# A two-layer graph network on one core: loads alternated at the end of layer 1, evictions taken first, and the counts' second part moved from GpSimd to VectorE

## The chip, the core and the metric

The kernel runs on one core of one Trainium2 chip. The core has TensorE (PE, matrix products into PSUM), VectorE (DVE), ScalarE (ACT), GpSimd (POOL), and SyncE (SP), which here issues nearly all DMA transfers. Each engine works through its own list of instructions in order and waits on semaphores; the DMA engines, 16 of them, are shared. The metric is device microseconds of one execution, lower is better.

## What is computed

`x` has 2500 rows of 1024; there are 80000 edges with a source, a target (sorted) and a weight.

```python
edge_index = jnp.stack([src, dst])
h = jnp.maximum(_layernorm(x), 0.0)
x = x + segment_sum((h @ W0)[src] * edge_weight[:, None], dst)      # layer 1
h = jnp.maximum(_layernorm(x), 0.0)
# layer 2: row, col = src, dst with one self loop for each node
h = einsum('nd,od->no', h, W1) + b
deg = zeros(N).at[row].add(1.0)
norm = deg[row] ** -0.5 * deg[col] ** -0.5
x = x + segment_sum(norm[:, None] * h[col], row)
```

## The kernel before

Both sums over edges are done as dense products. From the edge list the kernel builds two matrices of 2500 x 2500: the weighted adjacency of layer 1 and the edge counts of layer 2. Float32 accuracy comes from pairs of float16 numbers, a first part and what is left over, so each product is three matmuls.

**Quads.** A tile is 128 rows of the result; there are T = 20. A tile's matrix rows are built in 8 quads of 16 rows (QPT = 8, 160 quads in all). For a quad, POOL writes the fields of its edges (`fields_of`, `own_step`), DVE turns them into one-hot columns (`one_hots`, four instructions), PE multiplies these (L1695) into a PSUM pair that holds counts and weights. Then comes the eviction: ACT's `window_out` (L1413 to L1415) reads three pieces out of PSUM, DVE's `second_part` adds the self loop (L1118, which signals `c_self`) and forms the second part of the weights (L1119, L1122). PE may reuse the PSUM pair once L1119 has signalled `win_evac`. The counts are then handled in three steps: POOL adds them to the degrees (`sum_counts`, L774), ACT writes their first part (`counts_first`, L1420, signals `c_hi`), and POOL subtracts it to get the second part (`counts_left`, L779, signals `c_lo`). SP stores both parts to DRAM (`c_scratch`), to be read back transposed in layer 2.

**Stages.** (1) Support: 20 steps of `h @ W0` on PE; in the 16 steps w = 0 to 15 from step 4 on, one quad each is built beside them and parked in DRAM by SP (`park_quad`). SP also stores the split weights of layer 2 there (`store_w1`; ACT's `split_block` L1448 waits for an earlier one of these stores before it overwrites the staging buffer), and DVE takes the moments of x (`support_share`, L867). (2) The loop over tiles: PE adds up tile td (`dense`, L1796, 120 matmuls in 8 pieces) and builds the quads of tile td + 1 between the pieces. Up to quad 63 a window holds 2 rows (r = 2, six such tiles in the loop), after that 4 (r = 4, eleven tiles). DVE does the one-hots of quad n, then the second part of quad n - 1, then at q = 2 `residual` and at q = 4 `moments_of_x1`, then `further`, which loads a register from `quad_tab` (L1069) and branches. (3) The seam: after the last tile SP waits for the stores of the counts, issues five transposing loads of the counts' first parts (`load_first_parts`, L581), then stores a tile of x1, then loads x1 in groups of four tiles (`load_x1`, L591), and later two transposing loads of the second parts (`load_second_parts`, L586). ACT normalises each x1 tile (L1604), DVE splits it (L1297), and PE's `sums_of_first` (L1883) takes x1 tile k with quarter k // 4 of the transposed counts. Over on POOL the degrees are written to DRAM (L844, 2560 single numbers of 4 bytes) and read back in another layout (L847); DVE needs them at its ninth split. (4) Layer 2: five chunks of 500 rows on PE.

What sets the order is the text of each engine's program; nothing is scheduled by a planner. A wait holds everything behind it on its engine, and SP's transfers go out in SP's order.

Of the kernel before, what the change touches and what calls it, by code (L numbers as in the profile page):

```python
# [6 lines left out]
def gnn_two_layers(nc, x, src, dst, edge_weight, w0, w1, b1, out):  # L7
    f32, i32, f16 = mybir.dt.float32, mybir.dt.int32, mybir.dt.float16
    ALU = mybir.AluOpType
# [60 lines left out]
    with ctx:  # L70
# [394 lines left out]
        def _(sp):  # L465
# [59 lines left out]
            for w in range(PQ):  # L525
# [96 lines left out]
            sp.wait_ge(agg_ready, T)  # L622
# [57 lines left out]
        def _(pool):  # L680
# [95 lines left out]
            def counts_left(n, s, first_parts, second_parts):  # L776

                pool.wait_ge(c_hi, n + 1)
                pool.tensor_tensor(second_parts, by_source(c_stage(s)), first_parts, ALU.subtract).then_inc(c_lo, 1)  # L779

            def counts_of(n, td, q, first=False):

                sum_counts(n, q % CST)
                if not first:
                    last_left(n - 1, (q - 1) % QPT)

            def last_left(n, q):

                at = slice(q % QH * RQ, (q % QH + 1) * RQ)
                half = c_half(q // QH)  # L790
                counts_left(n, q % CST, half[:, 0, :, at], half[:, 1, :, at])

            def early_sum(n):
                sum_counts(n, n % 2)

            def early_left(n):
                counts_left(n, n % 2, c_parts[:, 0], c_parts[:, 1])

            pool.wait_ge(more_consts, 3)
            fields_of(0)  # L800
            for t in range(STEP0, T):
# [3 lines left out]
                if w < PQ:  # L805
                    if w > 0:
                        early_sum(w - 1)
# [5 lines left out]
                    if w > 0:  # L813
                        early_left(w - 1)
# [3 lines left out]
            early_sum(PQ - 1)  # L818
            early_left(PQ - 1)

            def own_tile(td, r, first=False):

                for q in range(QPT):
# [5 lines left out]
                    counts_of(n, td, q, first=first and q == 0)  # L829

            own_tile(PRE, 2, first=True)
# [1152 lines left out]
```

## Time and profile before

| | us |
|---|---|
| median of 3 runs | 1503.33 |
| lowest, highest | 1501.31, 1504.87 |
| the profiled execution | 1509.67 |
| its span, first to last instruction | 1507.9 |
| PE busy | 1422.7 (94%) |
| DVE busy | 896.9 (59%) |
| ACT busy | 507.4 (34%) |
| POOL busy | 453.9 (30%) |

All durations come from that one profiled execution. Busy PE is no measure of PE at its peak, but idle PE on the chain that ends last is time lost. Idle time of another engine costs nothing unless PE waits for it.

### The profile page before, as it was taken

To read this page: it belongs to the slowest core of one execution; us is meant where nothing else is said; L and a number is where in the kernel's file an instruction comes from. 1 tells how busy PE (TensorE), PEld (TensorE's weight loads), DVE (VectorE), ACT (ScalarE), POOL (GpSimd) and SP (SyncE) were. 2 spreads that over 40 slices of the span, in tenths; PEclk is the share of its full clock that TensorE was granted. 3 is DMA by queue.
4 is the path that set the end of the run, shared out by engine and by line. 5 is a ranking of instruction groups with operands and counts; after the bars stand their busy time and mean duration, and the time that the engine had idled before them with its cause. 6 is when DMAs were issued, how large, how long until landed. Compare 5 with 4: busy or idle time off the path is not lost.

```text
span 1507.9 us, 23949 instructions
## 1 busy us (share of the span) xinstructions
PE 1422.7 (94%) x7586; PEld 845.5 (56%) x7587; DVE 896.9 (59%) x1804; ACT 507.4 (34%) x922; POOL 453.9 (30%) x867
## 2 busy tenths in 40 slices
PE   3989988999999999999999994799999999999999
PEld 2445444556666666666666662346546446446455
DVE  7787775653767776776677760784452452452542
ACT  7545555532444444555455440710000000000000
POOL 2246444642555555555555540000000000000000
PEclk9989999999999999999999997899999999999999
DMA  8302424151434545545454559926308109108002
GB/s 304 113 20 47 102 47 90 20 90 49 96 78 80 85 78 103 94 80 102 85 95 84 103 88 101 304 73 131 119 1 206 44 1 209 40 21 201 28 2 82
DMA packets 422945, 139.17 MB, mean 92 GB/s; under 512 B 392832, under 2 KB 405120, under 8 KB 422796
## 3 DMA queue, kind: packets, MB, share of 16 engines
q1 hardware_dynamic: 422588, 137.41, 41.9%
q8 instruction: 60, 0.98, 0.3%
q0 software_dynamic: 208, 0.04, 0.2%
q14 instruction: 89, 0.73, 0.2%
HBM read 53.46 MB, written 53.52 MB: 71 GB/s over the span
## 4 chain that ended last, share of the span: by engine, by line
PE 72%; issue 8%; DVE 7%; SPq 4%; DMA 4%; POOL 3%; ACT 2%; POOLq 1%; ACTq 0%; DVEq 0%
PE pair L1796 24%; PE pair L1883 23%; PE pair L1943 13%; PE pair L1683 7%; PE pair L1695 4%; SPq L581 2%; DMA h<-in_x 1%; DMA w_scratch<-aux 1%; DVE stats L867 1%; SPq L508 1%; DMA h<-x_scratch 1%; DVE slots L1051 1%; POOL deg_acc L774 1%; DVE own_w L1360 1%; POOL fbuf L767 0%
## 5 line engine op out<-in xcount | busy, mean ns | idle before, releaser
L1796 PE MATMUL pair<-h,area 128*128 128x512 f16 x2400 | 542.7, 379 | 0.0
L1796 PEld LDWEIGHTS pair<-h,area 128*128 128x128 f16 x2400 | 342.6, 146 | 147.5
L1883 PE MATMUL pair<-area,h 128*128 128x500 f16 x1600 | 340.7, 376 | 30.7 <-DVE h L1297 30.7
L1883 PEld LDWEIGHTS pair<-area,h 128*128 128x128 f16 x1600 | 157.2, 98 | 213.5 <-issue 34.8
L774 POOL TENSOR_TENSOR deg_acc<-deg_acc,area 128x320 f32<-128x320 f32 x160 | 139.5, 872 | 273.3 <-DVE area L1118 271.8
L1943 PE MATMUL pair<-wmat,area 128*125 128x512 f16 x960 | 209.0, 379 | 0.0
L1617 ACT ACTIVATE area<-pair,sc 128x500 f16<-128x500 f32 x40 | 27.1, 677 | 452.4 <-PE pair L1883 452.4
L1413 ACT ACTIVATE area<-pair 128x320 f32<-128x320 f32 x160 | 70.0, 438 | 318.1 <-PE pair L1695 310.7
L1943 PEld LDWEIGHTS pair<-wmat,area 128*125 128x125 f16 x960 | 130.7, 137 | 75.5
L779 POOL TENSOR_TENSOR aux<-area,aux 128x320 f16<-128x320 f32 x144 | 147.7, 1026 | 0.0
L1695 PE MATMUL pair<-slots 128*128 128x120 f16 (+1 forms) x1152 | 112.9, 235 | 23.6 <-DVE area L1119 12.2
L1420 ACT ACTIVATE aux<-area 128x320 f16<-128x320 f32 x144 | 126.6, 879 | 0.0
L1695 PEld LDWEIGHTS pair<-slots 128*128 128x128 f16 x1152 | 84.9, 99 | 71.2 <-DVE slots L1055 23.8
L1049 DVE TENSOR_TENSOR slots<-iota_r,fbuf 128x320 f16<-128x320 f16 (+1 forms) x145 | 66.2, 456 | 93.2 <-POOL fbuf L768 47.5
L1683 PE MATMUL pair<-wmat,aux 128*128 128x512 f16 x480 | 116.4, 392 | 3.1 <-DVE wmat L943 3.1
L1683 PE MATMUL pair<-wmat,xt 128*128 128x512 f16 x480 | 113.9, 388 | 0.4 <-DVE h L956 0.3
L1122 DVE TENSOR_TENSOR area<-area 128x320 f16<-128x320 f16 x160 | 109.7, 686 | 5.5
L1340 DVE SCALAR_TENSOR_TENSOR area<-pair,sc,area 128x500 f16<-128x500 f32 x40 | 29.5, 739 | 128.9 <-ACT area L1617 128.9
L1051 DVE TENSOR_TENSOR slots<-iota_r,fbuf 128x1024 f16<-128x1024 f16 x145 | 101.0, 696 | 0.0
L1118 DVE TENSOR_TENSOR area<-area 128x16 f16 (+1 forms) x160 | 32.1, 200 | 101.8 <-ACT area L1415 99.6
L1683 PEld LDWEIGHTS pair<-wmat,aux 128*128 128x128 f16 x480 | 46.5, 100 | 54.2 <-issue 8.6
L1119 DVE SCALAR_TENSOR_TENSOR area<-pair,area 128x320 f16<-128x320 f32 x160 | 76.6, 479 | 0.0
(210 smaller groups left out, 1254.9 us busy)
## 6 DMA issues: line engine op xcount, KB each, us to landing
c_scratch<-aux SPq DMA_DIRECT2D x72, 320.0 KB, 4.5
xt<-in_x SPq DMA_DIRECT2D x19, 512.0 KB, 3.5
x_scratch<-xt SPq DMA_DIRECT2D x19, 512.0 KB, 4.7
xt<-x_scratch SPq DMA_DIRECT2D x20, 448.0 KB
out_x<-xt SPq DMA_DIRECT2D x19, 448.0 KB
h<-x_scratch SPq DMA_DIRECT2D x4, 2048.0 KB, 17.2
h<-in_x SPq DMA_DIRECT2D x5, 1024.0 KB, 7.8
h<-in_L_gnn_W SPq DMA_DIRECT2D x4, 1024.0 KB, 11.1
```

The lines of the kernel that those rows point to most:

```text
L774: pool.tensor_tensor(deg_acc[:], deg_acc[:], c_stage(s), ALU.add).then_inc(win_sum, 1)
L779: pool.tensor_tensor(second_parts, by_source(c_stage(s)), first_parts, ALU.subtract).then_inc(c_lo, 1)
L1051: nc.vector.tensor_tensor(part(to, 0, P), columns(8, P), by_touch(s, 1, 8, P), ALU.is_equal)
L1119: nc.vector.scalar_tensor_tensor(by_window(parts[:, 1], r), sums_in(pair, r, 1), A_DOWN, by_window(parts[:, 0], r), ALU.mult, ALU.subtract ...
L1122: nc.vector.tensor_tensor(parts[:, 1], parts[:, 1], seconds, ALU.add).then_inc(win_lo, 1)
L1413: act.activation(by_window(c_stage(s), r), sums_in(pair, r, 0), ACT.Copy, scale=C_DOWN)
L1420: act.activation(to, by_source(c_stage(s)), ACT.Copy).then_inc(c_hi, 1)
L1683: last = pe.matmul(dest[:, half * H:(half + 1) * H], h_t(t)[:, q, k, :], wmat[:, r, k, half * H:(half + 1) * H], start=k == q == r == 0, s ...
L1695: return pe.matmul(dest, touches[:, t, 0:P], touches[:, t, P:], start=first, stop=last, skip_group_check=True)
L1796: last = pe.matmul(sum_pair(e)[:, half * H:(half + 1) * H], wts(e)[:, q, :, k], hpart(k, r)[:, half * H:(half + 1) * H], start=k == q == r ...
L1883: ins = pe.matmul(sums_of(c, f), hpart(k, q)[:, f * P:(f + 1) * P], counts, start=first and q == 0, stop=last and q == 1, skip_group_check ...
L1943: last = pe.matmul(out_pair(m)[0:RW, half * H:(half + 1) * H], agg_of(k, q)[:, b * RW:(b + 1) * RW], wmat[:, r, k, half * H:(half + 1) * H ...
```

## The change

- `counts_left` leaves POOL and becomes DVE's: in the loop it follows the next quad's second part (`left_of(n - 2, q - 2)`), with two of them at a tile's end; in the support stage it is `early_left(w - 1)` just ahead of `early_second_part(w)`.
- DVE's order in a support step: quad w's second part now comes in step w, ahead of moments and selections, and the first one-hots of quad w + 1 come ahead of it. Before, it came in step w + 1. ACT's square roots (`std`) follow its `window_out` there.
- At a tile's end DVE does the last second part ahead of the next tile's first one-hots, and ACT the last first part inside the same tile.
- SP: the counts' parking is split off as `park_counts` and comes behind the weight stores and x loads of the step. At the seam the tile of x1 is stored first, the two degree transfers are SP's and not POOL's, and the loads of first parts and of x1 alternate.

```diff
@@ SP
                 sp.wait_ge(win_lo, n + 1)
                 for z in range(2):
                     sp.dma_start(a_dram[z, n], parked[:, z]).then_inc(a_out, 16)
+
+            def park_counts(n):
+
                 sp.wait_ge(c_lo, n + 1)
...
+                if w > 0:
+                    park_counts(w - 1)
             sp.wait_ge(sup_out, T)
             sp.dma_start(xt[:, 0, :], x[0:P, :]).then_inc(xt_in[0], 16)
             park_quad(PQ - 1)
+            park_counts(PQ - 1)
...
             sp.wait_ge(agg_ready, T - 1)
+            store_x1(last, 0)
+            sp.wait_ge(deg_ready, 1)
+            sp.dma_start(deg_dram.rearrange("t p -> p t"), deg[:, 0:T], allow_slow_non_contiguous=True).then_inc(deg_out, 16)
             sp.wait_ge(win_lo, NQ)
             sp.wait_ge(c_out[0], 32 * (PQ + T - PRE))
             sp.wait_ge(c_out[1], 32 * (T - PRE))
-            for j in range(HJ):
-                load_first_parts(0, j)
-            store_x1(last, 0)
+            load_first_parts(0, 0)
             for s in range(2):
                 sp.wait_ge(x1_out[s], 16 * last)
             for k in range(4):
                 sp.wait_ge(sup_free, k + 1)
                 load_x1(k)
+                load_first_parts(0, k + 1)
+                if k == 0:
+                    sp.wait_ge(deg_out, 16)
+                    flat = deg_dram.rearrange("t p -> (t p)")
+                    sp.dma_start(deg[0:RW, T:2 * T], flat[0:N].rearrange("(t p) -> p t", p=RW),
+                                 allow_slow_non_contiguous=True).then_inc(degu_in, 16)
@@ DVE
+            def counts_left(n, s, first_parts, second_parts):
+
+                dve.wait_ge(c_hi, n + 1)
+                nc.vector.tensor_tensor(second_parts, by_source(c_stage(s)), first_parts, ALU.subtract).then_inc(c_lo, 1)
...
+                    if q > 1:
+                        left_of(n - 2, q - 2)
...
                 n = QPT * (td + 2)
+                second_part(n - 1, r, quad_of(1 - e, QPT - 1), second_of(1), win_pair(1), c_stage((QPT - 1) % CST), td + 1, QPT - 1)
+                left_of(n - 2, QPT - 2)
                 own_hots(n + PRE_STEPS - PQ if r == 2 else (QPT // 2) * (td + 2) + QB // 2 + PRE_STEPS - PQ, 0,
                          n - 1 + PRE_STEPS - PQ if r == 2 else steps_used(n - 2), after)
-                second_part(n - 1, r, quad_of(1 - e, QPT - 1), second_of(1), win_pair(1), c_stage((QPT - 1) % CST), td + 1, QPT - 1)
+                left_of(n - 1, QPT - 1)
...
             for w in range(PQ):
-                if w > 0:
-                    hots_of(w, 0, 1)
-                    early_second_part(w - 1)
-                    hots_of(w, 1, 2)
+                hots_of(w, 1, 2) if w > 0 else None
                 sup_left(w + STEP0 - 1)
                 hots_of(w, 2, 8)
                 for g in W1_AT.get(w + STEP0, ()):
                     split_left(g)
-                support_share(w)
                 if w + STEP0 == HOTS_AT:
                     chunk_one_hots()
+                further(w, 2)
+                if w + 1 < PQ:
+                    hots_of(w + 1, 0, 1)
+                if w > 0:
+                    early_left(w - 1)
+                early_second_part(w)
+                support_share(w)
@@ ACT
                 if 0 <= w < PQ:
-                    if w in MOMENTS_AT:
-                        std(MOMENTS_AT[w])
                     if w > 0:
                         early_counts_first(w - 1)
                     early_window_out(w)
+                    if w in MOMENTS_AT:
+                        std(MOMENTS_AT[w])
```

POOL loses `counts_left` in both stages and the two degree transfers.

How it moves instructions, at three places. In these rows a name in brackets is a semaphore that is waited for.

SP in the support stage, two steps, of before: a quad's weights parked (L505), its counts (L508), then the weight stores of layer 2 (L496).

```order
L505 DMA a_scratch<-area 128x320 [waits win_lo]
L505 DMA a_scratch<-area 128x320
L508 DMA c_scratch<-area 128x20x16 [waits c_lo]
L508 DMA c_scratch<-area 128x20x16
L496 DMA w_scratch<-aux 128x2x512 [waits wlo_ready] x2
```

The same place of after:

```order
L505 DMA a_scratch<-area 128x320 [waits win_lo]
L505 DMA a_scratch<-area 128x320
L496 DMA w_scratch<-aux 128x2x512 [waits wlo_ready] x2
L511 DMA c_scratch<-area 128x20x16 [waits c_lo]
L511 DMA c_scratch<-area 128x20x16
```

The wait for `c_lo` and the two stores of counts have moved behind the weight stores.

DVE in the r = 2 part of the loop, the end of a tile, of after (L1028 to L1034 are the one-hots, L1097 to L1101 the second part, L1106 the moved subtraction):

```order
L1097 TENSOR_TENSOR area<-area 128x16 [waits win_act]
L1098 SCALAR_TENSOR_TENSOR area<-pair,area 128x320
L1101 TENSOR_TENSOR area<-area 128x320 [waits win_evac]
L1105 REGISTER_ALU
L1106 TENSOR_TENSOR aux<-area,aux 128x20x16 [waits c_hi]
L1043 ISA
L428 REGISTER_ALU [waits own_fields]
L1028 TENSOR_TENSOR slots<-iota_r,fbuf 128x8x40 [waits step_used]
L1030 TENSOR_TENSOR slots<-iota_r,fbuf 128x8x128
L1032 REGISTER_ALU
L1033 TENSOR_TENSOR slots<-slots,fbuf 128x8x40 [waits hots_plain]
L1034 TENSOR_TENSOR slots<-slots,fbuf 128x8x40
```

and a quad inside a tile of before, from its one-hots to the register load of `further`:

```order
L1049 TENSOR_TENSOR slots<-iota_r,fbuf 128x8x40 [waits step_used,own_fields]
L1051 TENSOR_TENSOR slots<-iota_r,fbuf 128x8x128
L1053 REGISTER_ALU
L1054 TENSOR_TENSOR slots<-slots,fbuf 128x8x40 [waits hots_plain]
L1055 TENSOR_TENSOR slots<-slots,fbuf 128x8x40
L1116 REGISTER_ALU
L1118 ISA [waits win_act]
L1118 TENSOR_TENSOR area<-area 128x16
L1119 SCALAR_TENSOR_TENSOR area<-pair,area 128x320
L1122 TENSOR_TENSOR area<-area 128x320 [waits win_evac]
```

A wait for `c_hi` and one more instruction have come behind each second part, and at a tile's end the one-hots stand behind the last second part.

SP at the seam, of before:

```order
L581 DMA_TRANSPOSE area<-c_scratch 128x4x512 [waits c_out0,c_out1,win_lo,agg_ready]
L581 DMA_TRANSPOSE area<-c_scratch 128x4x512 x4
L557 DMA x_scratch<-xt 128x1024 [waits x1_ready]
L591 DMA h<-x_scratch 128x4x1024 [waits sup_free,x1_out1,x1_out0]
L591 DMA h<-x_scratch 128x4x1024 [waits sup_free] x3
L591 DMA h<-x_scratch 128x3x1024 [waits x1_out0,agg_ready]
```

and of after:

```order
L563 DMA x_scratch<-xt 128x1024 [waits x1_ready,agg_ready]
L619 DMA deg_scratch<-deg 128x20x1 [waits deg_ready]
L587 DMA_TRANSPOSE area<-c_scratch 128x4x512 [waits c_out1,c_out0,win_lo]
L597 DMA h<-x_scratch 128x4x1024 [waits sup_free,x1_out1,x1_out0]
L587 DMA_TRANSPOSE area<-c_scratch 128x4x512
L633 DMA deg<-deg_scratch 125x20x1 [waits deg_out]
L597 DMA h<-x_scratch 128x4x1024 [waits sup_free]
L587 DMA_TRANSPOSE area<-c_scratch 128x4x512
L597 DMA h<-x_scratch 128x4x1024 [waits sup_free]
L587 DMA_TRANSPOSE area<-c_scratch 128x4x512
```

The first x1 load has one transposing load ahead of it and not five, and both degree transfers have come into SP's list: the write ahead of every transposing load, the read ahead of the second x1 load.

## Rows read from the trace of the kernel before

**Rows 1.** Windows: length, busy us by engine (instructions), clock, DMA share, GB/s.

```profile
170.00:210.00 40.00, 33.66 (x223) 17.83 (x221) 32.27 (x68) 18.76 (x31) 18.68 (x46) 0.96 0.30 59
210.00:252.00 42.00, 33.69 (x221) 17.77 (x220) 25.08 (x63) 22.98 (x37) 18.20 (x51) 0.96 0.46 94
```

**Rows 2.** The chain that ended last, support stage: start, us, what.

```profile
197.15 0.78 POOL area L779
...
199.76 4.42 DMA w_scratch<-aux
...
233.45 7.83 DMA h<-in_x
...
248.09 0.98 PE pair L1695 x8
```

**Rows 3.** Waits of PE, 60 to 330 us: total, times, longest.

```profile
PE pair L1695 <- DVE area L1119: 12.2, 4, 5.9
```

**Rows 4.** Timeline of the r = 2 loop: start, us, instruction, idle before it.

```profile
454.24 0.86 POOL L774 TENSOR_TENSOR deg_acc<-deg_acc,area 128x320 f32<-128x320 f32 x1 [2.37 <-DVE area L1118]
...
455.06 1.02 POOL L779 TENSOR_TENSOR aux<-area,aux 128x320 f16<-128x320 f32 x1
...
456.50 0.33 DVE L1049 TENSOR_TENSOR slots<-iota_r,fbuf 128x320 f16<-128x320 f16 x1 [1.22 <-POOL fbuf L768]
...
457.82 0.18 DVE L1118 TENSOR_TENSOR area<-area 128x16 f16 x1
...
458.43 0.70 DVE L1122 TENSOR_TENSOR area<-area 128x320 f16<-128x320 f16 x1
```

**Rows 5.** The chain, whole span: a tile's last piece of 25 matmuls.

```profile
508.46 5.42 PE pair L1796 x25
...
539.39 5.41 PE pair L1796 x25
...
568.59 5.40 PE pair L1796 x25
```

**Rows 6.** Timeline, 882 to 1010 us: two DVE instructions.

```profile
889.47 0.49 DVE L1049 TENSOR_TENSOR slots<-iota_r,fbuf 128x640 f16<-128x640 f16 x1 [0.85 <-issue]
...
896.40 0.81 DVE L1258 TENSOR_REDUCE deg<-deg_acc 128x20 f32<-128x320 f32 x1
```

**Rows 7.** Windows over the seam, columns as in rows 1.

```profile
920.00:940.00 20.00, 1.43 (x7) 0.71 (x5) 0.00 (x0) 0.00 (x0) 3.02 (x1) 0.67 1.21 139
940.00:960.00 20.00, 7.83 (x26) 3.13 (x27) 8.84 (x15) 11.54 (x11) 0.00 (x0) 0.57 1.01 392
```

**Rows 8.** Timeline of the seam.

```profile
897.79 1.54 POOL L844 DMA_DIRECT2D deg_scratch<-deg  x1 [3.50 <-DVEq L1260]
...
900.51 36.41 SPq L581 DMA_TRANSPOSE area<-c_scratch  x5
...
952.17 58.14 PE L1883 MATMUL pair<-area,h 128*128 128x500 f16 x263 [30.74 <-DVE h L1297]
```

**Rows 9.** The chain across the seam and behind it.

```profile
937.66 10.62 DMA h<-x_scratch
...
952.17 70.17 PE pair L1883 x320
```

**Rows 10.** DMA issues, 880 to 1010 us: KB each, median us from issue to landing.

```profile
wmat<-w_scratch SPq DMA_TRANSPOSE x1, 24.5
deg_scratch<-deg POOLq DMA_DIRECT2D x1, 10.0 KB, 24.4
deg<-deg_scratch POOLq DMA_DIRECT2D x1, 9.8 KB, 15.5
```

**Rows 11.** All 25 issues of L581: issue ns min/median/max, then landing us.

```profile
L581 SPq DMA_TRANSPOSE area<-c_scratch x25: 1882/2257/13646, 900.5 to 1361.0; - x25
...
DMA to landing us min/median/max: 4.4/4.8/23.2
```

**Rows 12.** All 72 issues of L522, 2560 pieces of 128 bytes each: landing us.

```profile
DMA to landing us min/median/max: 3.4/4.5/5.7
```

More of the change, by code:

```diff
@@ L774, in sum_counts @@
                 pool.tensor_tensor(deg_acc[:], deg_acc[:], c_stage(s), ALU.add).then_inc(win_sum, 1)
[L776 to L797, printed above, removed]
             pool.wait_ge(more_consts, 3)
@@ L806, in _ @@
                     if w > 0:
-                        early_sum(w - 1)
+                        sum_counts(w - 1, (w - 1) % 2)
                     if w + 1 < PQ:
@@ L817, in _, with own_tile @@
                     pool.memset(h[:, T - 1, :], 0.0).then_inc(pad_done, 1)
-            early_sum(PQ - 1)
-            early_left(PQ - 1)
-            def own_tile(td, r, first=False):
+            sum_counts(PQ - 1, (PQ - 1) % 2)
+            def own_tile(td, r):
                 for q in range(QPT):
@@ L828, in own_tile @@
                         own_step((QPT // 2) * td + q // 2 + 1 + QB // 2 + PRE_STEPS - PQ, (q // 2 + 1) % 2)
-                    counts_of(n, td, q, first=first and q == 0)
-            own_tile(PRE, 2, first=True)
-            with pool.Fori(PRE + 1, QB // QPT) as td:
+                    sum_counts(n, q % CST)
+            with pool.Fori(PRE, QB // QPT) as td:
                 own_tile(td, 2)
@@ L840, in _ @@
                              of=PRE_STEPS if q == QPT - 2 else None)
[L841 to L848 removed]
+                sum_counts(QPT * td + q, q % CST)
         @block.vector
@@ L1122, in second_part, with left_of, early_left @@
                 nc.vector.tensor_tensor(parts[:, 1], parts[:, 1], seconds, ALU.add).then_inc(win_lo, 1)
+            def counts_left(n, s, first_parts, second_parts):
+                dve.wait_ge(c_hi, n + 1)
+                nc.vector.tensor_tensor(second_parts, by_source(c_stage(s)), first_parts, ALU.subtract).then_inc(c_lo, 1)
+            def left_of(n, q):
+                at = slice(q % QH * RQ, (q % QH + 1) * RQ)
+                half = c_half(q // QH)
+                counts_left(n, q % CST, half[:, 0, :, at], half[:, 1, :, at])
+            def early_left(n):
+                counts_left(n, n % 2, c_parts[:, 0], c_parts[:, 1])
             def early_second_part(n):
@@ L1428, in early_window_out, with tile, first_of @@
                 window_out(n, n % 2, 2, 2, parked[:, 0], early_second, WIN)
-            def tile(td, e, r, before=True):
+            def tile(td, e, r):
+                def first_of(n, p):
+                    b = p // QH
+                    if p % QH == 0:
+                        act.wait_ge(c_out[b], (32 * PQ if b == 0 else 0) + 32 * (td + 1 - PRE))
+                    counts_first(n, p % CST, c_half(b)[:, 0, :, p % QH * RQ:(p % QH + 1) * RQ])
                 for q in range(QPT):
@@ L1436, in tile @@
                     window_out(n, q % CST, r, CST, quad_of(1 - e, q)[:, 0], second_of(q % 2), win_pair(q % 2))
-                    if q > 0 or before:
-                        p = (q - 1) % QPT
-                        b = p // QH
-                        if p % QH == 0:
-                            act.wait_ge(c_out[b], (32 * PQ if b == 0 else 0) + 32 * (td + 1 - PRE))
-                        counts_first(n - 1, p % CST, c_half(b)[:, 0, :, p % QH * RQ:(p % QH + 1) * RQ])
+                    if q > 0:
+                        first_of(n - 1, q - 1)
+                first_of(n, QPT - 1)
             def split_block(g):
@@ L1578, in _ @@
                 act.wait_ge(w_out[k], 16 * KD)
-            tile(1, 1, 2, before=False)
+            tile(1, 1, 2)
             tile(2, 0, 2)
```

14 lines of the change are left out of this document (1 added, 13 removed).

## The prediction
> **What bounds the kernel now.** I first read the windows of busy time over the whole span. In the r = 4 part of the loop and in layer 2 PE goes from matmul to matmul, so nothing can be won there but by shorter PE work, and the change has none. PE idles in three places, and each was then followed in the chain that ended last, in the waits and in the timeline.
>
> The first is the support stage. From 170 to 252 us PE is busy 33.66 and 33.69 us of 40 and 42, so it idles 6.3 + 8.3 = 14.7 us [rows 1]. 12.2 us of PE's waits in this stage are for DVE's L1119, the release of the PSUM pair [rows 3]. The chain shows why it is late: POOL's subtraction L779, then SP's stores, then a weight store of 4.42 us to its landing, then ACT and DVE; later a load of x that SP issued only behind all this, 7.83 us, at whose end PE resumes at 248.09 [rows 2]. So the eviction of a quad hangs on a subtraction that nobody there needs, because SP and ACT work in order.
>
> The second is the r = 2 part of the loop. From 508.46 to 539.39 a tile takes 30.93 us, or 3.87 per quad; the next one, r = 4, takes 29.20 [rows 5]. In the r = 2 timeline DVE stands idle 1.22 us before its one-hots, waiting for POOL, and POOL has just spent 1.02 us on L779 [rows 4]. The loop that sets the pace is DVE L1118, POOL L774, POOL L779, POOL's copies, DVE's one-hots. From 456.50 to 457.82 these take 1.32 us, and L1122 starts 0.61 after L1118 [rows 4].
>
> The third is the seam. PE is busy 1.43 us of the window from 920 and resumes at 952.17 [rows 7, 8]: 30.7 us idle. ACT's first x1 group, issued at 937.66, landed 10.62 us later [rows 9]; SP had spent 36.41 us from 900.51 on five transposing loads ahead of it [rows 8]. Undisturbed, such a load takes 2.26 us to issue and 4.8 to land [rows 11]. Here everything is slow together: a weight transpose took 24.5 us, and so did (24.4) the degree write, issued at 897.79, which puts its landing at 922.2; the degree read after it took 15.5 [rows 8, 10]. The size of the pieces alone isn't it: the count stores, also 2560 pieces but of 128 bytes and far apart, land in 4.5 [rows 12]. I read it as the 4-byte numbers, all in 10 KB of DRAM, holding up the others.
>
> **Support stage.** The wait for `c_lo` goes behind the weight stores and the x loads on SP, the subtraction goes to DVE, and DVE evicts quad w ahead of moments and selections. The 14.7 us [rows 1] lose their cause. Against it: DVE is busy 32.27 us of 40 [rows 1], gets an instruction more, and now waits inside step w for quad w's last matmul and ACT's eviction, with moments and selections pushed between that and the next quad's second one-hots. Those are four steps with moments and eight with selections; I charge 3.7 us for them, as a guess between 0 and 10 us. ACT's square root now comes after DVE's late moments, and ACT's next work queues behind it; PE is a whole support step away from that, so nothing is charged. Gain 11 us; bounds 4 (14.7 less the 10) and 16 (14.7 and the clock, 0.96 in both windows, back to 1).
>
> **Loop, r = 2.** Without L779 POOL's loop falls below 3 us and DVE's own becomes the longest. How long is the moved instruction on DVE? The trace has none, but L1258 reads the same strided view of 320 numbers in 0.81 us [rows 6]; dense float16 of that size takes 0.33 [rows 4], POOL 1.02. I take 0.81. Behind L1122 DVE's sequencer loads a register: L1049 came after 0.85 us of idle at the end of a 0.70 us L1122, so 1.55 from start to start [rows 6]. The new instruction hides in that gap, but its wait and dispatch lengthen it by some 0.15. A quad costs 1.32 + 0.61 + 1.70 = 3.63 us, eight 29.0. At q = 2 and q = 4 the gap was already filled by residual and moments, so there the instruction and the longer fill show, about 1.0 each, and two subtractions at the tile's end show 0.4: 31.4 us. That is 0.5 more than 30.93, times six tiles +3 us. Bounds: with 0.33 us nothing shows and PE's 29.2 holds, -10; with 1.02 us +8. I keep +2, a little below the sum, because the first part's POOL wait also goes from the tile end.
>
> The Trainium skill ("VectorE: DVE Perf Modes", the section on the TRN2 errata) gives a float32 `tensor_tensor` as (N + 151)/0.96 ns, which by estimate is 0.49 us for 320 numbers; by it the r = 2 tiles would come out at about 30.3 us and the stage 4 us faster, not 2 slower. The strided L1258 at 0.81 speaks against using it here, and no run yet shows which holds.
>
> **Loop, r = 4.** A tile is PE's 29.20 us [rows 5]. DVE has 28 us or so to do, by the same sum with one-hots only every second quad. The tight place is the tile's end: the next tile's one-hots now follow the last second part. PE works 5.4 us on its last piece [rows 5]; DVE needs an estimated 1.3 until ACT has evicted, 0.61, 0.62 for L1122, 0.81, and 1.8 for the wider one-hots (1.32 and three times 0.16, from L1049's 0.49 and 0.33 [rows 4, 6]): 5.1 us. It just fits. I charge 1 us for eleven tiles; bounds 0 and +7 (0.6 us each).
>
> **The seam.** In the new order SP stores the counts about 1 us later (two subtractions stand behind each other on DVE), loads the last weights, stores x1 and issues the degree write near 903.5, an estimate from 900.51 [rows 8] and these. If the write holds up the queue as before, for some 21 us, it ends near 925. Part of the first transposing load trickles in meanwhile and lands at 927. One x1 group follows, 2.1 MB at 392 GB/s [rows 7] or 5.3 us: 932. From the landing at 948.28 to PE at 952.17 it took 3.9 us [rows 8, 9], so PE resumes near 936, not 952: 16 us won. Then the read of degrees, 15.5 us [rows 10], stands ahead of the second x1 group, which lands about 948; PE needs it split by 936 + 14 = 950, at 14.0 us a group (70.17 / 5 [rows 9]), and has it near 952 to 956. I charge 4. Seam: -12 us. Later groups come every 10 us or so and PE takes 14; the rest is hidden.
>
> **The sum.** -11 + 2 + 1 - 12 = -20 us. The profiled execution took 1509.67 us with a span of 1507.9, 6 above the median; 20 off the median of 1503.33 gives **1483 us**. Its own range, with the small bounds, is 1474 to 1493.
>
> **The rivals.**
> 1. *The write holds up nothing when SP issues it.* For it: the count stores land in 4.5 us from the same queue [rows 12], and the slow write was POOL's only one of its kind. Against it: what stood still were SP's transfers, not POOL's. Then the first loads are in by about 915, PE resumes at its own end, 921.4, and 31 us are won for 12: 1464 us.
> 2. *Support stage wins nothing.* DVE's wait for quad w takes the place of PE's wait for the release, and PE waits for one-hots instead. For it: DVE 81% busy. Against it: PE's idle time is tied to the chain of SP, not to DVE's load. 1494 us.
> 3. *DVE sets the pace of the loop.* If the moved instruction takes 1.02 us or meets POOL's L774, r = 2 gives +8 and r = 4 +7: 1503.33 - 11 + 15 - 12 = 1495; with the low support gain of 4, 1502.
> 4. *The degree read blocks SP's queue: slower.* It has 125 rows of 20 numbers, all single, and stands ahead of three quarters of x1; the kernel itself cuts other 125-row transfers into 112 and 13. If it runs on a few DMA engines, say five, each has 500 numbers. The read before took 15.5 us for some 156 per engine, 0.10 us each, and the write 24.4 for 160, 0.15 [rows 10]: 50 us, up to 76. With 50 the second group lands at 988, PE starts on it at 992 and ends the sums at 1048, against 952.17 + 70.17 = 1022.3: +26 where I have -12. 1503.33 - 8 + 26 = 1521 us. It decides from a read of some 32 us on: then the seam loses the 8 us which the rest wins.
>
> The Trainium skill ("DMA: Bandwidth & Descriptors", the section on why a DMA increments its semaphore by 16) says that a transfer from SP runs on the largest number of engines up to 16 that divides the slowest dimension, which is five for 125 rows. If it holds, rival 4's premise stands, though not its price per number. No transfer shown here tells it.
>
> **How the numbers follow.** Forecast 0.45; rival 1 0.20; rival 2 0.10; rival 3 0.15; rival 4 0.10. About 0.2%, 3 us, is what a measurement of this kernel can tell from no change. The range 1458 to 1502 us takes in rivals 1 to 3 and leaves out rival 4 and the far ends of the rest. Faster by over 0.2% 0.86, within 0.04 (the upper end of rival 3), slower 0.10 (rival 4).
>
> **What would show it.** Support: the wait of L1695 for the second part below 3 us, a weight store never between POOL and ACT in the chain, PE's idle time from 170 to 252 us near 4. Loop: the moved instruction at 0.7 to 0.9 us; r = 2 tiles at 31 to 31.5 us with DVE and no longer POOL named before PE's gaps, r = 4 at 29.2 to 29.4. Seam: the degree write landing after 20 us or more and PE resuming near 936 with a short second gap; a landing within 6 us is rival 1, a gap of over 30 us before x1's second group rival 4. The forecast is wrong if the seam is off by more than 8 us in either direction, or if r = 4 tiles grow.

## The result and the profile after

| | before | after |
|---|---|---|
| median us | 1504.43 | 1499.85 |
| lowest, highest | 1501.31, 1509.06 | 1497.14, 1502.39 |
| span of the profiled execution | 1507.9 | 1498.6 |

The ratio is 0.997, 95% interval 0.9957 to 0.9983: the change wins 4.6 us, with 2.6 to 6.5 inside the interval, where 20 had been forecast. The two profiled spans differ by 9.3 us; the profile of before lies some 5 us above its median, so sizes below are taken from timed runs where there are some, and from the traces for the place.

By stages the traces give: first tiles 3.7 us earlier, r = 2 the same, r = 4 slower by 7.8, and the seam shorter by 13.4 (from the end of the last dense piece to the 144 matmuls of layer 2 in a row behind it).

**Support stage.** The windows that answer to [rows 1]:

```profile
170.00:210.00 40.00, 35.20 (x230) 18.63 (x229) 35.15 (x75) 20.84 (x34) 17.32 (x44) 0.91 0.33 50
210.00:252.00 42.00, 42.00 (x288) 23.05 (x287) 28.96 (x66) 26.68 (x42) 22.35 (x59) 1.00 0.39 76
```

PE's idle time in these two windows falls from 14.7 to 4.8 us, and the wait of [rows 3] is gone. What PE waits for at its window matmuls, 60 to 330 us, is now the one-hots (L1034 in after):

```profile
PE pair L1697 <- DVE slots L1034: 12.6, 4, 4.9
```

In before PE waited 12.2 us there for the second part and 4.5 for one-hots, 16.7 together, so the waits of the stage as a whole fall by only 4.1. One of the four, 2.98 us at 104.88, is in before as well. The longest of the four is new, from PE's timeline:

```profile
298.93 0.98 PE L1697 MATMUL pair<-slots 128*128 128x120 f16 x8 [4.87 <-DVE slots L1034]
```

DVE's timeline tells what it did meanwhile. L1098 is the eviction of quad 12; L1218 to L990 is `later_windows`, a table for the loop; L1028 begins quad 13's second one-hots:

```profile
284.44 0.34 DVE L1028 TENSOR_TENSOR slots<-iota_r,fbuf 128x320 f16<-128x320 f16 x1 [5.84 <-POOL fbuf L771]
...
286.60 0.48 DVE L1098 SCALAR_TENSOR_TENSOR area<-pair,area 128x320 f16<-128x320 f32 x1
...
287.35 0.68 DVE L1218 CAST area<-area 1x768 f32<-1x768 int32 x1
...
296.39 1.23 DVE L990 TENSOR_TENSOR area<-area 1x768 int32<-1x768 f32 x1
297.50 0.30 DVE L1028 TENSOR_TENSOR slots<-iota_r,fbuf 128x320 f16<-128x320 f16 x1
```

The table takes 10.2 us. Before the change it stood ahead of an eviction; now it stands between one and the next one-hots, while DVE had just been idle for 5.84 us.

Two more of the four waits, 1.60 us at 181.21 and 3.10 at 193.99, have something else in common. Ahead of both a one-hot instruction that has a median of 0.32 us took 2.2, and it ended together with POOL's L737, which ran beside it:

```profile
177.45 2.62 POOL L737 TENSOR_TENSOR xt<-h,xt 128x1024 f16<-128x1024 f32 x1 [9.60 <-ACT xt L1468]
...
178.00 2.26 DVE L1033 TENSOR_TENSOR slots<-slots,fbuf 128x320 f16<-128x320 f16 x1
...
190.52 2.33 POOL L737 TENSOR_TENSOR aux<-h,aux 128x1024 f16<-128x1024 f32 x1 [4.01 <-ACT aux L1468]
...
190.79 2.24 DVE L1033 TENSOR_TENSOR slots<-slots,fbuf 128x320 f16<-128x320 f16 x1
```

Ahead of the second of them DVE also had a block of selections, 3.8 us from 185.96. Before has such long one-hots too (2.25 us at 116.26, 130.84 and 180.44, among others), so they are no effect of the change; no run here moves L737, so that it is the cause is not shown, and what it costs was not measured.

**The loop.** The moved instruction, from the groups of DVE instructions:

```profile
L1106 DVE TENSOR_TENSOR aux<-area,aux 128x320 f16<-128x320 f32 x144 | 116.0, 805 | 0.0
```

At r = 2, from 382 to 535 us, DVE no longer waits for POOL ahead of its one-hots. In before that was

```profile
DVE slots L1049 <- POOL fbuf L768: 32.6, 28, 1.2
```

and in after

```profile
DVE slots L1028 <- POOL fbuf L781: 0.5, 1, 0.5
```

In its place DVE has more to do: it is busy 141.1 us of these 153 and not 113.7. One has eaten up the other. Five tiles, from the first to the last r = 2 piece, take 156.4 us in both kernels.

The last pieces of r = 4 tiles in the chain, to be compared with [rows 5]:

```profile
564.86 5.39 PE pair L1798 x25
...
625.67 5.39 PE pair L1798 x25
...
685.68 5.39 PE pair L1798 x25
...
745.70 5.40 PE pair L1798 x25
```

Two tiles take 60.8, 60.0 and 60.0 us where before two took 58.4. PE waits at every second tile's start only (five times, 5.8 us in all), where DVE's loop, whose body holds two tiles, goes round. The timeline there:

```profile
598.98 0.81 DVE L1106 TENSOR_TENSOR aux<-area,aux 128x320 f16<-128x320 f32 x1
...
605.59 0.49 DVE L1028 TENSOR_TENSOR slots<-iota_r,fbuf 128x640 f16<-128x640 f16 x1 [5.81 <-issue]
...
607.50 0.48 DVE L1098 SCALAR_TENSOR_TENSOR area<-pair,area 128x320 f16<-128x320 f32 x1
...
608.11 0.58 PE L1697 MATMUL pair<-slots 128*128 128x240 f16 x4 [2.03 <-DVE area L1098]
```

Nothing that the profile shows was waited for in those 5.81 us; in the chain they hold two stretches called issue, of 2.30 and 2.28 us (1.3 to 2.1 each at the later boundaries). The kernel before has the same gap at the same place, and PE loses nothing by it:

```profile
663.51 0.49 DVE L1049 TENSOR_TENSOR slots<-iota_r,fbuf 128x640 f16<-128x640 f16 x1 [4.54 <-issue]
```

What differs is where the gap begins. In before DVE's last instruction ahead of it ends 3.0 us after PE's last piece has begun (658.97 against 655.96), in after 5.9 (599.79 against 593.88).

**The seam.** The timeline of SP, and PE's resuming, which answer to [rows 8]:

```profile
903.73 0.51 SPq L563 DMA_DIRECT2D x_scratch<-xt  x1
904.29 0.43 SPq L619 DMA_DIRECT2D deg_scratch<-deg  x1
905.20 11.57 SPq L587 DMA_TRANSPOSE area<-c_scratch  x1
916.88 0.51 SPq L597 DMA_DIRECT2D h<-x_scratch  x1
917.44 12.96 SPq L587 DMA_TRANSPOSE area<-c_scratch  x1
930.45 0.48 SPq L633 DMA_DIRECT2D deg<-deg_scratch  x1
930.97 3.65 SPq L597 DMA_DIRECT2D h<-x_scratch  x1
934.52 55.48 PE L1885 MATMUL pair<-area,h 128*128 128x500 f16 x256 [8.99 <-DVE h L1296]
```

The degree write landed after 18.6 us. PE's gap is 8.99 us where it was 30.7. Behind it PE is busy throughout until 990, but then waits 3.2 and 4.0 us more; before had no such waits there. The granted clock from 1010 to 1025 us, behind them, is 0.81.

### The profile page after: what moved, and what is told of

The parts are those of the page before. It is cut to its first block, busy times and chain, and to the rows that moved or that the text cites. A ratio compares the mean times of both kernels' runs of the same rounds, so it can differ in the third digit from the quotient of the medians.

```text
span 1498.6 us, 24031 instructions
## 1 busy us (share of the span) xinstructions
PE 1426.0 (95%) x7586; PEld 845.8 (56%) x7587; DVE 1000.8 (67%) x1964; ACT 509.6 (34%) x922; POOL 356.6 (24%) x705
## 4 chain that ended last, share of the span: by engine, by line
PE 55%; issue 20%; DVE 9%; POOL 5%; SPq 5%; POOLq 2%; DMA 1%; ACT 1%; DVEq 1%
PE pair L1885 18%; PE pair L1798 17%; PE pair L1945 13%; SPq L587 3%; PE pair L1697 3%; PE pair L1685 3%; DVE own_w L1359 2%; POOL fbuf L781 2%; POOLq L766 1%; POOL fbuf L769 1%; POOL fbuf L771 1%; SPq L592 1%; POOL deg_acc L787 1%; DVE stats L846 1%; DVE slots L1033 1%
## 5 line engine op out<-in xcount | busy, mean ns | idle before, releaser
L1885 PE MATMUL pair<-area,h 128*128 128x500 f16 x1600 | 339.7, 375 | 12.2 <-DVE h L1296 9.0
L1619 ACT ACTIVATE area<-pair,sc 128x500 f16<-128x500 f32 x40 | 27.1, 677 | 450.1 <-PE pair L1885 450.1
L1106 DVE TENSOR_TENSOR aux<-area,aux 128x320 f16<-128x320 f32 x144 | 116.0, 805 | 0.0
L1101 DVE TENSOR_TENSOR area<-area 128x320 f16<-128x320 f16 x160 | 107.9, 674 | 5.5
L1028 DVE TENSOR_TENSOR slots<-iota_r,fbuf 128x320 f16<-128x320 f16 (+1 forms) x145 | 56.6, 391 | 69.7 <-POOL fbuf L771 27.6
L1098 DVE SCALAR_TENSOR_TENSOR area<-pair,area 128x320 f16<-128x320 f32 x160 | 76.5, 478 | 0.0
L1685 PEld LDWEIGHTS pair<-wmat,xt 128*128 128x128 f16 x480 | 46.1, 99 | 52.0 <-issue 4.3
## 6 DMA issues: line engine op xcount, KB each, us to landing
h<-x_scratch SPq DMA_DIRECT2D x4, 2048.0 KB, 10.3
```

What stands on the lines that cost most here:

```text
L1098: nc.vector.scalar_tensor_tensor(by_window(parts[:, 1], r), sums_in(pair, r, 1), A_DOWN, by_window(parts[:, 0], r), ALU.mult, ALU.subtract ...
L1101: nc.vector.tensor_tensor(parts[:, 1], parts[:, 1], seconds, ALU.add).then_inc(win_lo, 1)
L1106: nc.vector.tensor_tensor(second_parts, by_source(c_stage(s)), first_parts, ALU.subtract).then_inc(c_lo, 1)
L1685: last = pe.matmul(dest[:, half * H:(half + 1) * H], h_t(t)[:, q, k, :], wmat[:, r, k, half * H:(half + 1) * H], start=k == q == r == 0, s ...
L1885: ins = pe.matmul(sums_of(c, f), hpart(k, q)[:, f * P:(f + 1) * P], counts, start=first and q == 0, stop=last and q == 1, skip_group_check ...
```

## The experiments

A line "start of tiles" below is the time from the first of PE's transposes in the support stage to the first 25-matmul piece; it takes out that the traces begin up to 2 us apart.

**1. The seam alone.** The kernel before, with this at the seam and POOL's two degree transfers taken out:

```diff
-            for j in range(HJ):
-                load_first_parts(0, j)
             store_x1(last, 0)
+            sp.wait_ge(deg_ready, 1)
+            sp.dma_start(deg_dram...)
...
+            load_first_parts(0, 0)
...
                 load_x1(k)
+                load_first_parts(0, k + 1)
```

> The kernel before with the seam of after alone: x1's tile stored first, both degree transfers from SP, loads of first parts and of x1 alternating. Theory (the three parts add up, the seam wins its 13 us by itself): 1504.4 - 13 = 1491 us, the support stage and the loop as in the kernel before to within 1 us, PE resuming at 9 us after its last dense piece. Rival (the seam wins only because the loop before it ends later and so hides part of the degree write, 4 us): 1495 us, and the gap of PE 13 us or more.

1493.19 us, ratio 0.9922 (0.99 to 0.9943), halfway between theory and rival; PE's gap of 9.40 us is the theory's. The seam wins 11 us by itself. So the rest of the change loses 6.7.

**2. The table ahead.** `later_windows` moved ahead of `further` in its step:

```diff
+                if w + STEP0 == TABLE_AT:
+                    later_windows()
                 further(w, 2)
...
-                if w + STEP0 == TABLE_AT:
-                    later_windows()
```

> After, with the table of the later windows (13 instructions, 10.2 us on DVE) moved ahead of further and of the next quad's first one-hots in step w = 12, where DVE stands idle 5.84 us. Theory (the stall of 4.87 us at 298.9 and the low clock behind it are this table, standing between quad 12's eviction and quad 13's second one-hots): the stall goes, the support stage ends 5 to 6 us earlier, 1499.9 - 5.5 = 1494.4 us. Rival (DVE's load as a whole is the limit of this stage, the table only shows it first): the stall moves to the next step or two, and 1 us or less is won, 1499.

1493.42 us, ratio 0.9929 (0.9907 to 0.9952), 6.4 us below after. The stall of 4.87 us is replaced by two short ones in PE's timeline:

```profile
287.73 0.59 PE L1697 MATMUL pair<-slots 128*128 128x120 f16 x8 [0.67 <-DVE area L1098]
...
291.99 0.59 PE L1697 MATMUL pair<-slots 128*128 128x120 f16 x8 [1.08 <-DVE slots L1034]
```

Start of tiles: 321.3 and 321.0 us in before and the first experiment, 314.9 to 317.5 in the kernels with after's support stage (after itself is the highest), 309.9 here. With the table out of the way the support stage wins 11 us in this trace. The three kernels further down that have the same edit start their tiles at 309.5, 310.7 and 313.2, so a single trace gives this size to some 3 us; the 6.4 us are timed.

**3. The tile's end.** The next tile's one-hots ahead of the last second part again:

```diff
+                own_hots(...)
                 second_part(n - 1, ...)
                 left_of(n - 2, QPT - 2)
-                own_hots(...)
                 left_of(n - 1, QPT - 1)
```

> After, with the tile's end of the kernel before in DVE's order: the next tile's one-hots ahead of the last second part, the two subtractions last; they stay on DVE. Theory (the r = 4 loop lost 7.8 us because the tile's end is too long ahead of the loop's branch: four one-hot instructions now stand between the last eviction and the rest): nothing of the one-hots' 1.8 us is waited for behind the last eviction, 3 to 6 us come back, 1494 to 1497 us. Rival (the end's order is of no matter, what counts is what DVE has to do before its branch, the last subtraction with its wait for ACT): 1500 us, each second tile still 1 us or more over 29.2.

1497.31 us, ratio 0.9954 (0.9935 to 0.9974), its interval overlapping with after's. In the trace four waits for L1098 of 5.3 us in all remain at the boundaries (after: five, 5.8 us). The order of the end is not the cause, or only a small part: r = 4 as a whole is 0.8 us shorter than in after.

**4. No loop.** DVE's r = 4 tiles written out one after the other, the same instructions:

```diff
-            with dve.Fori(j + 1, last) as j:
+            for j in range(j + 1, last):
```

> After, with DVE's loop over the r = 4 tiles written out (ten tiles in a row, no branch back); all else, and all instructions of each tile, as in after. Theory (the loss sits at every second tile's end only, where DVE branches back and is idle 5.8 us before it goes on): the stalls of 1.2 to 2.0 us at each second boundary vanish, r = 4 takes 377 to 378 us and not 384.4, 1499.9 - 7 = 1493 us. Rival 1 (DVE simply has too much to do at a tile's end): the stalls stay and spread over all boundaries, 1500. Rival 2 (straight code must be fetched too, and costs DVE more than one branch): stalls at other places, 1500 or slower.

1489.6 us, ratio 0.991 (0.9885 to 0.9935), 10 us below after. The chain:

```profile
562.25 5.40 PE pair L1798 x25
591.43 5.40 PE pair L1798 x25
620.61 5.40 PE pair L1798 x25
```

29.18 us for each tile, no wait at a boundary. With the same work at each tile's end the loss is gone, so DVE's load alone is not the cause; the way round the loop is. The DMA lists show a queue of instructions, number 14: 95 packets over the whole of after, 89 in before, 77 here. The Trainium skill ("Runtime: NRT & Kernel Launch", the section "Instruction fetch mechanics") says that a taken branch out of the window of prefetched instructions forces a fetch before the engine goes on; that agrees with an idle DVE of 5.8 us that waits for nothing, and with its vanishing here. That each of the two stretches of 2.3 us is one such fetch is argued, not shown; what is shown is that the idle time belongs to the loop.

**5. DVE's second part first.** At q = 1 of an r = 4 tile, `second_part` ahead of `own_hots`, still in the loop:

```diff
                         elif q % 2 == 1 and q < QPT - 1:
+                            if q == 1:
+                                second_part(n - 1, ...)
                             own_hots(...)
-                        second_part(n - 1, ...)
+                        if r == 2 or q != 1:
+                            second_part(n - 1, ...)
```

> After, with DVE taking the second part of quad 0 ahead of the one-hots at q = 1 in the r = 4 tiles; the loop stays a loop. Theory (PE waits at every second tile for this one instruction, which stands 1.8 us of one-hots behind the end of DVE's branch): the waits for L1098 vanish or fall below 0.3 us each, r = 4 takes 379 us or less, not 384.4, 1499.9 - 6 = 1494 us. Rival (the one-hots are as urgent, and PE waits for them at the next quad instead): waits of the same 1 to 2 us, now for L1034, 1499 to 1501 us.

1502.24 us, ratio 0.9988 (0.9977 to 0.9999). The theory's remedy failed, as the rival said. The idle time stands where it stood, and PE waits for the one-hots, five times and 9.7 us in all in the r = 4 part:

```profile
602.84 0.19 DVE L1097 TENSOR_TENSOR area<-area 128x16 f16 x1 [5.62 <-ACT area L1418]
...
606.03 0.58 PE L1701 MATMUL pair<-slots 128*128 128x240 f16 x4 [2.50 <-DVE slots L1034]
```

The profile names ACT's L1418 for it, but that eviction had ended at 598.94 in the timeline: the 3.9 us behind it are again the way round. Both things that PE needs stand behind the branch, and neither order of the two helps.

**6. The subtraction back on POOL in the loop.** POOL has `last_left` of before again, DVE neither `left_of` nor the new tile's end; support stage and seam stay.

```diff
-                    if q > 1:
-                        left_of(n - 2, q - 2)
...
+                    if not (first and q == 0):
+                        last_left(n - 1, (q - 1) % QPT)
```

> After, with the counts' subtraction back on POOL in the loop alone and DVE's and POOL's orders there as in the kernel before; the support stage and the seam are after's. Theory (the loop won nothing by the move at r = 2 and lost 7.8 us at r = 4): the r = 4 tiles take 29.2 to 29.3 us again, the r = 2 part the same 156.4 us as in both kernels, 1499.9 - 7.8 = 1492 us. Rival (POOL and DVE each pace r = 2 and the move did win something there that another cost hides): r = 2 grows by 2 us or more, 1494 or above.

1488.26 us, ratio 0.9901 (0.988 to 0.9923): 11.6 us below after, where 8 had been expected. From 500 to 915 us PE waits 0.6 us in all:

```profile
PE pair L1706 <- DVE slots L1047: 0.6, 2, 0.4
```

DVE is still idle 4.08 us at the same boundary, but its last instruction ahead of that ends at 593.0, which is 3.0 us after PE's last piece has begun and not 5.9, and the one-hots behind it start at 597.1: the way round is covered by PE's long piece. From the start of the last r = 2 piece to the start of the last tile's dense block it takes 350.2 us, as in before; after has 358.0. Another 3.4 us lie in the seam (81.9 us from the end of the last dense piece to the first product, 85.3 in after). Over the traces of the first six experiments this stretch varies between 82 and 85 us with PE's gap, 6.2 to 9.6; why was not separated.

The five tiles of r = 2 take 156.4 us here and in the unrolled kernel too: 31.3 a tile, whoever subtracts. DVE waits for POOL again, 32.4 us of it.

**7. Degrees as rows.** PE turns the degrees (a transposition of 128 x 20), DVE copies them to SBUF, SP writes 20 rows of 512 bytes behind the first transposing load:

```diff
-            sp.dma_start(deg_dram.rearrange("t p -> p t"), deg[:, 0:T], ...)
...
+            sp.wait_ge(deg_rows_ready, 1)
+            sp.dma_start(deg_dram, deg_rows).then_inc(deg_out, 16)
...
+                if g == 2:
+                    pe.wait_ge(deg_ready, 1)
+                    pe.transpose(bank[0][0:T, P:2 * P], deg[:, 0:T], ident[:, :])
```

> After, with the degrees turned by PE (128 x 20 to 20 x 128, after the third piece of the last tile), copied by DVE and stored as 20 rows of 512 bytes behind the first transposing load, in the place of 2560 single numbers. Theory (the 2560 four-byte pieces hold up every transfer of the queue for some 19 us): the write lands within 5 us, no transposing load takes over 4 us to issue before x1 arrives, PE's gap at the seam falls from 9 us to 2 or less; behind it the order of the last loads limits the gain: 1499.9 - 9 = 1491 us, down to 1488. Rival (the transposing loads are slow by themselves at this place, whatever is written beside them, since x1 and weights move too): the gap stays at 7 us or more, 1498 or above.

1487.37 us, ratio 0.9874 (0.9848 to 0.99), 12.5 below after, more than expected: beside PE's gap the wait of 3.2 us at the end of the sums is gone as well. Windows of after, then of this kernel (columns as in rows 1):

```profile
905.00:923.00 18.00, 18.00 (x86) 12.04 (x85) 1.41 (x7) 0.33 (x2) 0.00 (x0) 1.00 0.89 58
923.00:935.00 12.00, 3.01 (x14) 1.71 (x13) 1.83 (x2) 4.25 (x4) 0.00 (x0) 0.81 0.90 217
```

```profile
905.00:923.00 18.00, 18.00 (x86) 11.99 (x85) 4.29 (x14) 5.06 (x7) 0.00 (x0) 1.00 0.89 217
923.00:935.00 12.00, 12.00 (x58) 6.15 (x57) 10.77 (x18) 7.03 (x7) 0.00 (x0) 1.00 1.01 329
```

In the same 18 us the DMA engines are as busy, 0.89 of their time, but move 217 GB/s and not 58. Ten KB in single numbers had kept them occupied, and PE's gap is gone altogether. The edit also puts the write behind the first transposing load, which took 2.48 us to issue here; size of the pieces and place were not tried apart. Experiment 8, where the single numbers go out 6 us earlier and still jam the first transposing load, speaks for the pieces.

**8. Degrees on POOL's queue.** After, with the two degree transfers issued by POOL as in before:

```diff
-            sp.dma_start(deg_dram.rearrange("t p -> p t"), deg[:, 0:T], ...)
+            pool.dma_start(deg_dram.rearrange("t p -> p t"), deg[:, 0:T], ...)
```

> After, with the degrees' write and read on POOL's queue again, as 2560 single numbers; the loads still alternate. Theory (the write holds up the transfers of all queues while it lasts, whoever issues it; SP's issue of it only made it no better): PE's gap at the seam stays at 8 to 10 us, 1498 to 1501 us; all of the seam's gain is then the alternation of loads and none the move of the degrees. Rival (on SP's own queue it also blocks what stands behind it): PE's gap is 4 us or less, 1494 us.

1508.05 us, ratio 1.0031 (1.0006 to 1.0056), and wide, 1497.9 to 1519.8. The profiled execution has the gap as expected:

```profile
931.18 29.11 PE L1885 MATMUL pair<-area,h 128*128 128x500 f16 x129 [9.35 <-DVE h L1296]
```

The write landed in 17.1 us from POOL, 18.6 from SP, the transposing load beside it took 14.0 us to issue, and PE's gap is 9.35 against 8.99: in this execution the write's queue doesn't matter for the jam. The median 8 us above after was expected by neither side, and its cause isn't settled; the one execution that was profiled (1500.66) is among the shortest. Over all runs the move to SP's queue does seem to be worth something. The trace has one sign of it, in the read of the degrees: from POOL it took 20.2 us to land, the two transposing loads beside it took 10.5 and 13.1 us to issue, and PE's wait at the end of the sums is 5.9 us. In after, the transposing loads behind SP's read took 7.3 and 7.0, and that wait is 3.2. Whether this makes the 8 us was not tested.

**9. Second parts and bias first.**

```diff
+            for j in range(LJ):
+                load_second_parts(0, j)
             sp.wait_ge(agg_ready, T)
+            sp.dma_start(bias_b, ...).then_inc(b_in, 16)
             sp.wait_ge(x1_out[0], 16 * (T // 2))
             load_x1(4)
```

> After, with the two transposing loads of second parts and the bias ahead of x1's last group, not behind the last tile's load. Theory (DVE's norms wait 9.4 us for the bias, and with them PE at the end of the sums, 3.2 + 4.0 us): norms start 10 us earlier or more, both waits of PE go, 1499.9 - 7 = 1493 us. Rival (x1's last tiles come later and PE waits for them): the wait moves ahead by some 20 us and grows, 1500 us or slower.

1501.41 us, ratio 0.9987 (0.9973 to 1.0002): nothing won. DVE's norms (L1357) start to 0.01 us at the time of after, 987.71, though the last dense piece ended 1.2 us earlier, and for another reason:

```profile
986.58 1.23 DVE L1296 TENSOR_TENSOR h<-aux,h 128x1024 f16<-128x1024 f32 x1
987.72 0.47 DVE L1357 TENSOR_SCALAR own_w<-area,dinv 128x500 f32<-128x500 f16 x1
```

x1's last tiles now load later, and the last split stands ahead of the norms on DVE. The wait for the bias had been named rightly, but a second one was right behind it. The rival has the time and the late tiles, but PE's wait at this place did not grow: 2.73 us and not 3.21.

**10. Four together:** experiments 2, 4, 7 and 9.

> Four edits of after together: the later windows' table first, DVE's r = 4 loop written out, the degrees stored as 20 rows, the second parts and the bias ahead of x1's last group. Theory (they are independent: 6.4 and 10.3 us measured by themselves, 9 and 7 expected): 1499.9 - 32 = 1468 us. Rival (in the seam the last two meet the same limit, SP's order, and add up to no more than the larger one): 1475 us.

1474.5 us, ratio 0.9802 (0.9778 to 0.9825). The sum by measured parts is 6.4 + 10.3 + 12.5 - 1.6 = 27.6 us, found are 25.4. The 1468 of the theory had counted 7 us for experiment 9, which won nothing. The rival's 1475 is met in number; no run shows whether for its reason.

**11. Three together, and the bias's wait.** Experiments 2, 6 and 7; then the same with DVE's wait for the bias at its first use:

```diff
-            dve.wait_ge(b_in, 16)
             for c in range(NCK):
...
+                if m == 0:
+                    dve.wait_ge(b_in, 16)
                 dve.wait_ge(xr_in[e], 32 * (m // 2 + 1))
```

> Three edits of after together: the later windows' table first, the counts' subtraction on POOL in the loop as in the kernel before, the degrees stored as 20 rows of 512 bytes. Theory (they sit in three different stages and add up as measured alone: 6.4, 11.6 and 12.5 us): 1499.9 - 30.5 = 1469 us. Rival (the seam gives some of it back, since the end of the loop comes earlier against the last weight loads and count stores): 1474 us.

> The same three edits, and DVE's wait for the bias stands at its first use (the end of the first chunk) and no longer ahead of the norms. Theory (with the stores as rows, the norms wait 9.4 us for the bias alone and keep the second parts of the sums from PE for 4.3 us): PE's wait for L1344 there falls to 2 us or less, 2.5 us less than the same kernel without this edit, 1466.5 us. Rival (the norms then wait for the second transposing load of second parts, as they did for x1's last tile where these loads stood first, and end at the same time): no difference.

1472.79 us (0.9794; 0.9778 to 0.9811) and 1464.47 us (0.9738; 0.9721 to 0.9754). The first misses its theory by 4 us and comes near its rival, 27.1 us won where the parts add up to 30.5; the second lies 2 us below its theory. It is the best kernel of this study, 35 us below after. Its timeline over the seam:

```profile
911.19 67.63 PE L1904 MATMUL pair<-area,h 128*128 128x500 f16 x320
...
978.66 10.52 PE L1964 MATMUL pair<-wmat,area 128*125 128x512 f16 x48
```

PE goes from dense pieces to sums to products without a wait of more than 0.5 us. The step from the first to the second kernel is 8.3 us by the medians, but the traces account for the 3.0 us wait of PE that is gone and no more; their spans are 1467.0 and 1464.3, and the first one's profiled execution is the fastest of its five. The rest of the 8.3 stays open.

## Why the prediction was right and wrong

- **The seam was right**, term and mechanism, but the close agreement is in part luck. Forecast -12, found -11 timed and -13.4 in the trace. The write holds up the queue (18.6 us, forecast about 21), and the degree read does not block: the second x1 group was issued right behind it at 930.97 and PE never ran dry on it, so the 4 us charged there were not lost. PE resumes at 934.5 (forecast 936), but from a loop that ends 4.1 us later than the forecast took it to. In experiment 1, where it ends as in before, PE resumes at 930.6: the gap shrank by 21.3 us and not by 16. The excess was lost again at the end of the sums, in waits of 3.2 and 4.0 us (4.3 and 1.2 in experiment 1), where the prediction had said "the rest is hidden". Rivals 1 and 4 were wrong.
- **The r = 2 term was right in its mechanism and small in its error.** Forecast +2, found 0. POOL's part in the pace went, and DVE's own order took its place. The instruction takes 0.805 us, as the strided row said and not the estimated 0.49 of the Trainium skill ("VectorE: DVE Perf Modes", the section on the TRN2 errata). But the sum of 31.4 us a tile compared itself with one tile of 30.93 [rows 5]. The mean of five was already 31.3 in before, since one of them takes 32.5, and the others stay at 30.9 to 31.0 in after: the 1.0 us charged at q = 2 and q = 4 each does not show. That the mean comes out near 31.4 is luck.
- **The support term failed in one step.** Of the 14.7 us 9.9 went, and the chain of SP's stores with them, but "moments and selections pushed between that and the next quad's second one-hots" were charged at 3.7 us, as a guess, and of these the one that matters was not looked up: `later_windows`, 10.2 us in one block, in the only step where it meets a quad's second one-hots. It cost 6.4 us timed; without it the stage gives 4.9 + 6.4 = 11.3, the forecast 11. The other waits for one-hots that are left (1.6 and 3.1 us) are of the size of the guess, and in their course PE waits for one-hots where it waited for the release, as rival 2 had said, though not for as long. The edits of the stage were right, the place of one call was not.
- **The r = 4 term failed, and it decided the case.** The step was "It just fits. I charge 1 us". The sum of 5.1 us out of 5.4 was right for what it summed: the one-hots are done 5.2 us after PE's last piece has begun (599.06 against 593.88), and PE takes them without a wait. It left out what stands behind them on DVE: the second of the two subtractions, 0.81 us, and the way round DVE's loop, 4.1 to 5.8 us in which DVE does nothing. In before that gap had been hidden in PE's last piece (4.54 us at 663.51, in the very trace that the prediction read). The new tile's end makes it begin 2.9 us later, and PE waits for what stands behind the branch. It cost 7.8 us by the trace, and 11.6 timed with what followed at the seam: as much as the seam won. The bound of +7 was too low, and rival 3, which named DVE in the loop, was near in time and had the wrong mechanism: not the pace of a quad, but one place in two tiles.

By the timed medians the parts are: seam -11.2 (experiment 1 against before), support -4.9 (experiment 6 against 1), loop +11.6 (after against experiment 6), together -4.5; measured -4.6. Each step starts from the kernel where the last one ended, so that they add up proves nothing; what they give is the share of each. The 3.4 us of seam in the loop's 11.6 are the least certain of it.

## What to carry to other kernels

Before work is moved to an engine with idle time, find out where that idle time lies, and look at each loop's end on its own: an engine's way round its loop can be hidden under another engine's long piece, and then the last instructions ahead of the branch have no slack, however idle the engine is on average. When evictions are moved forward in an order, list what now stands between them and the next urgent step, and look up the longest single block there. And where a small transfer lands late, look at the size of its pieces before its queue: 10 KB as rows instead of single numbers, and behind the first load, were worth more here than all that the change did.

## What the runs showed of the hardware

- DVE's way round a loop whose body is two tiles showed as 4.1 to 5.8 us of idle time in after and 3.4 to 4.6 in before, at most boundaries with nothing that it waited for; in straight code of ten tiles DVE had no gap longer than 1.6 us. The prediction reckoned with none.
- A transfer of 2560 pieces of 4 bytes kept the DMA engines 0.89 busy for 18 us at 58 GB/s and slowed the transposing loads beside it, from SP's or from POOL's queue alike: they took 11.6 and 13.0 us to issue in after, and 14.0 with the write on POOL's queue, instead of 2.2, the median of the 25 in after.
- A transposing load issued while 2 MB of x1 are under way takes about 7.3 us to issue even without that write (7.50, 7.32, 7.25, 7.43 us in experiment 7).
- A one-hot `tensor_tensor` of 128x320 float16 on DVE, 0.32 us by its median, took 2.24 and 2.26 us where POOL's `tensor_tensor` of 128x1024 (L737, 2.1 to 2.6 us) ran beside it, and ended with it.
